# A fused state-space and mixture-of-experts layer on one core: the chunk products, masks and norm in another order

## What is computed

```python
h  = rmsnorm(layernorm(x)) * w_norm_in
z, xx, B, C, dt_raw = split(h @ w_in_proj)          # 256, 256, 8x64, 8x64, 8
xx = silu(causal_conv4(xx) + conv_b)
dt = mean_per_head(softplus(dt_raw @ w_dt + b_dt))  # 8 heads
y  = ssd_scan(xx, dt, B, C, A_log) + xx * D         # state space scan, by chunks
x1 = x + layernorm(x) + rmsnorm(y * silu(z)) * w_norm_out @ w_out_proj
f  = layernorm(x1)
w, i = top_2(softmax(f @ gate_w + gate_b))          # of 4 experts
out = x1 + f + mean_of_2(shared experts(f)) + sum(w * routed experts(f)[i])   # relu, 128->512->128
```

## Time and profile before

| | us |
|---|---|
| median of 3 runs (575.18 to 577.2) | 575.23 |
| the profiled execution's own time | 571.37 |
| its span, first to last instruction | 569.6 |
| one body of the middle (from 322.11 to 387.88 on TensorE) | 65.8 |

### The profile page before, as it was taken

One profiled execution on the slowest core, in us unless ns is written; L12 is line 12 of the kernel. 1 busy time (PEld: TensorE's weight loads), 2 busy tenths in 40 slices (PEclk: granted clock), 3 DMA queues, 4 the chain that ended last, 5 costly groups with the idle time before them and its releaser, 6 DMA issues.

```text
span 569.6 us, 11656 instructions
## 1 busy us (share of the span) xinstructions
PE 541.9 (95%) x3912; PEld 428.5 (75%) x3912; DVE 437.3 (77%) x1037; ACT 355.9 (62%) x767; POOL 173.0 (30%) x232
## 2 busy tenths in 40 slices
PE   8887999999989999999999999999999999899996
PEld 7666778877877777877777777778777778777774
DVE  5868868978699777978778787987778777675654
ACT  4894579547675478636776387745886377752442
POOL 3074405520162203620155201622045211442011
PEclk9989999999999999999999999999999999999999
DMA  6650027200550006500371005600073004500030
GB/s 200 193 152 2 0 73 173 64 1 2 157 167 1 2 6 206 115 1 0 106 162 54 0 0 157 166 0 0 32 201 89 0 0 137 148 25 1 26 72 20
DMA packets 37353, 41.41 MB, mean 73 GB/s; under 512 B 3482, under 2 KB 27716, under 8 KB 37316
## 3 DMA queue, kind: packets, MB, share of 16 engines
q1 hardware_dynamic: 36724, 40.80, 26.1%
q10 hardware_dynamic: 592, 0.15, 0.1%
HBM read 37.79 MB, written 3.15 MB: 72 GB/s over the span
## 4 chain that ended last, share of the span: by engine, by line
PE 48%; DVE 20%; issue 9%; DMA 9%; ACT 8%; POOL 3%; SPq 2%; DVEq 0%; ACTq 0%; POOLq 0%
PE bank L425 7%; DMA grow<-lc_rows 6%; PE bank L427 5%; PE bank L426 5%; PE bank L534 4%; PE bank L639 4%; DVE cv L1122 4%; PE bank L640 4%; PE bank L641 4%; ACT act_h L871 3%; DVE act_l L1269 3%; PE bank L546 2%; PE bank L562 2%; ACT L968 2%; PE bank L556 2%
## 5 line engine op out<-in xcount | busy, mean ns | idle before, releaser
L1269 DVE SCALAR_TENSOR_TENSOR act_l<-bank,act_h 128x512 fp32r<-128x512 f32 x192 | 131.7, 687 | 66.2 <-ACT act_h L871 64.1
L871 ACT ACTIVATE act_h<-bank 128x512 fp32r<-128x512 f32 x192 | 114.3, 596 | 79.4 <-PE bank L427 75.7
L1493 POOL TENSOR_TENSOR late<-late 128x512 f32<-128x512 f32 x31 | 39.8, 1285 | 166.3 <-DVE late L1277 165.7
L425 PE MATMUL bank<-fTl,w1h 128*128 128x512 f32 x192 | 86.9, 452 | 1.2 <-DVE act_l L1269 0.5
L891 ACT ACTIVATE seg<-seg,lneg 128x128 f32<-128x128 f32 x256 | 81.2, 391 | 3.7 <-DMA seg<-lc_rows 3.7
L639 PE MATMUL bank<-act_l,w2h 128*128 128x512 f32 x192 | 77.6, 404 | 1.5 <-DVE act_l L1269 1.5
L640 PE MATMUL bank<-act_h,w2l 128*128 128x512 f32 x192 | 76.0, 396 | 0.0
L427 PE MATMUL bank<-fTh,w1h 128*128 128x512 f32 x192 | 75.7, 394 | 0.0
L641 PE MATMUL bank<-act_h,w2h 128*128 128x512 f32 x192 | 75.6, 394 | 0.0
L426 PE MATMUL bank<-fTh,w1l 128*128 128x512 f32 x192 | 75.5, 393 | 0.0
L1480 POOL TENSOR_TENSOR xw<-xs,seg 128x128 f32<-128x128 f32 x48 | 20.0, 416 | 153.0 <-ACT seg L891 87.5
(11 more groups left out here) (176 smaller groups left out, 1059.3 us busy)
## 6 DMA issues: line engine op xcount, KB each, us to landing
seg<-lc_rows SPq DMA_DIRECT2D x32, 512.0 KB, 4.2
late<-gk_rows SPq DMA_DIRECT2D x8, 1024.0 KB, 9.1
grow<-lc_rows SPq DMA_DIRECT2D x48, 128.0 KB, 4.8
x_in<-L_attn_hidden_dram SPq DMA_DIRECT2D x8, 256.0 KB, 4.1
out_dram<-late SPq DMA_DIRECT2D x8, 256.0 KB, 3.7
late<-L_ffn_sw_dram SPq DMA_DIRECT2D x2, 512.0 KB, 7.2
late<-L_ffn_rw_dram SPq DMA_DIRECT2D x1, 1024.0 KB, 7.7
CT<-L_attn_w_in_proj_dram SPq DMA_DIRECT2D x1, 512.0 KB, 5.4
```

Of the source, the lines that this page charges most:

```text
L425: mm(dst, stat_h, mov_l, start=True, stop=False)
L871: nc.scalar.activation(act_h[:, b % RING, :], HID[b % 2][:], ACT.Relu).then_inc(act_h_ready, 1)
L1269: v_.scalar_tensor_tensor(act_l[:, r, :], HID[b % 2][:], 0.0, f(act_h[:, r, :]), ALU.max, ALU.subtract)\
```

## The change

- TensorE: the gram of chunk 0 stays in slot 13; the gram of chunk c+1 is now issued in step 2 of chunk c, right before the y product of chunk c. The state product moves from step 2 to step 1 (slots 13, 16, 19). Slot 22 holds only `proj(s+1, 0)`.
- VectorE: chunk 0's masked halves stay in slot 13. Chunks 1 and 2 get theirs in step 0 (slots 15, 18), half 0 ahead of `act_low`, half 1 behind it; chunk 3 gets both in slot 21, ahead of `routed_out` and `act_low`. The state update moves to the end of slots 13, 16, 19. The norm's statistics of the next sequence stand ahead of `act_low` of slot 15, its rest behind it; `norm1_apply` moves behind `act_low` and half 1 of slot 18. The copy of B's third block moves from ScalarE to VectorE (slot 5), with a semaphore of its own.
- ScalarE: loses that copy; `growth` of chunk 1 moves from slot 12 to slot 14, behind `decays`.
- GpSimd: in slot 18 the first `add_term` waits for the next sequence's norm (`hn_ready`).
- SyncE: `segments(s, 1)` and `growth_rows(s, 1)` are issued ahead of the store of `older`.
- The opening keeps its own order on VectorE (both halves in step 1, the state in step 2), but takes the new order on TensorE, ScalarE's `growth` included.

```diff
@@ sync
+                    segments(s, 1)
+                    growth_rows(s, 1)
                 if older is not None:
                     sp_eng.wait_ge(out_ready, nth(older, 1, 1))
                     sp_eng.dma_start(out_dram[older], out_t).then_inc(out_stored, 16)
                 if s is not None:
-                    segments(s, 1)
-                    growth_rows(s, 1)
                     growth_rows(s, 2)
@@ tensor
-            def y_product(s, c):
-
+            def state_product(s, c):
                 if c > 0:
                     pe.wait_ge(state_step, nth(s, 8, (2, 5, 8)[c - 1]))
+                pe.wait_ge(btok_ready, nth(s, 3, c + 1))
+                pe.wait_ge(xw_ready, nth(s, 6, 2 * c + 2))
+                for n in range(NP):
+                    ins = mm(MAIN[1][:, n * 64:(n + 1) * 64], btok[:, at(n)], xw[:, n, :, :].rearrange("p t d -> p (t d)"),
+                             start=True, stop=True)
+                ins.then_inc(s_psum, 1)
+
+            def y_product(s, c):
+
+                if c == NCH - 1:
+                    pe.wait_ge(state_step, nth(s, 8, 8))
                 if c < NCH - 1:
...
+                    gram(s, c + 1, None)
...
-                    if b == 0:
+                    if b == 0 and c == NCH - 1:
                         pe.wait_ge(mg_ready, nth(s, 8, 2 * c + 2))
...
-                    if step == 1:
+                    if step == 1 and c == 0:
                         gram(s, c, prev)
-                        if c == NCH - 1 and not is_seq(s, n_seq - 1):
-                            proj(s + 1, 0)
+                    if step == 1 and c < NCH - 1:
+                        state_product(s, c)
+                    if step == 1 and c == NCH - 1 and not is_seq(s, n_seq - 1):
+                        proj(s + 1, 0)
@@ scalar
                         btok_copy(s, c)
-                        if c < NCH - 2:
-                            growth(s, c + 1)
+                        if c == 1:
+                            growth(s, 2)
...
+                    if step == 2 and c == 0:
+                        growth(s, 1)
...
-                    if s is not None and i == 5:
-                        b_copy(s, 2)
@@ vector
+            def third_b_copy(s):
+                dve.wait_ge(proj_psum, made(s, 8))
+                v_.tensor_copy(BT[:, 2, :], MAIN[0][:]).then_inc(b_third_ready, 1)
...
+                        if i in (15, 18, 21):
+                            masked_gram(s, i // 3 - 4, 0)
+                        if i == 15 and not is_seq(s, n_seq - 1):
+                            norm1_stats(s + 1)
+                        if i == 21:
+                            masked_gram(s, 3, 1)
...
+                    if s is not None and i == 5:
+                        third_b_copy(s)
                     if prev is not None and i in (15 + LAG, 19 + LAG):
                         routed_out(prev, (i - 15 - LAG) // 4)
                     if (new := block_at(i, prev, older)) and not (i == 0 and prev is not None):
                         act_low(*new)
...
+                    if s is not None and i in (15, 18):
+                        masked_gram(s, i // 3 - 4, 1)
+                    if s is not None and i in (13, 16, 19):
+                        next_state(s, i // 3 - 4)
+                    if s is not None and i == 15 and not is_seq(s, n_seq - 1):
+                        norm1(s + 1)
+                    if s is not None and i == 18 and not is_seq(s, n_seq - 1):
+                        norm1_apply(s + 1)
@@ gpsimd
+                    if prev is not None and s is not None and i == 16 + LAG and not last:
+                        pool.wait_ge(hn_ready, nth(s + 1, 4, 4))
                     if prev is not None and i in (16 + LAG, 19 + LAG):
                         add_term(prev, (i - 15 - LAG) // 4)
```

More of the change, by code:

```diff
@@ L221, in build @@
         b_ready = sem("b_ready")
+        b_third_ready = sem("b_third_ready")
         c_ready = sem("c_ready")
@@ L470, in proj @@
                     dst = MAIN[j - 10]
-                    last, k = ((b_ready, 3), (b_ready, 4), (xs_ready, 1), (xs_ready, 2))[j - 10]
-                    pe.wait_ge(last, nth(s, 2 if last is xs_ready else 4, k))
+                    last, per, k = ((b_third_ready, 1, 1), (b_ready, 3, 3), (xs_ready, 2, 1), (xs_ready, 2, 2))[j - 10]
+                    pe.wait_ge(last, nth(s, per, k))
                     if j == 12 and not is_seq(s, 0):
@@ L513, in b_tokens @@
                         pe.wait_ge(gate_logits, nth(prev, 4, 4))
-                    pe.wait_ge(b_ready, nth(s, 4, 4))
+                    pe.wait_ge(b_ready, nth(s, 3, 3))
+                    pe.wait_ge(b_third_ready, nth(s, 1, 1))
                     if is_seq(s, 0):
@@ L782, in opening @@
                         b_tokens(0, c, None, None)
-                    gram(0, c, None)
+                    if c == 0:
+                        gram(0, c, None)
                     if c < 2:
@@ L790, in opening @@
                         proj(1, 0)
+                    if c < NCH - 1:
+                        state_product(0, c)
                     y_product(0, c)
@@ L838, in b_copy @@
                 act.wait_ge(proj_psum, made(s, b + 6))
-                nc.scalar.copy(BT[:, b, :], MAIN[(b + 2) % 4][:]).then_inc(b_ready, 1)
+                nc.scalar.copy(BT[:, b, :], MAIN[(b + 2) % 4][:]).then_inc(b_third_ready if b == 2 else b_ready, 1)
             def c_copy(s, b):
@@ L1145, in c_copy @@
                 v_.tensor_copy(CT[:, b, :], MAIN[b][:]).then_inc(c_ready, 1)
-            def attend(s, c, step):
[L1148 to L1155, removed]
-                if step == 2:
[L1158 to L1174, removed]
@@ new lines, in masked_gram @@
+            def masked_gram(s, c, hf):
+                dve.wait_ge(g_psum, nth(s, 8, 2 * c + hf + 1))
+                dve.wait_ge(decay_masked, nth(s, 8, 2 * c + hf + 1))
+                if hf == 0 and (v := nth(s, 4, c)) is not None:
+                    dve.wait_ge(y_psum, v)
+                v_.tensor_tensor(mg[:, hf], MAIN[2 + hf][:].rearrange("p (n l) -> p n l", n=NP), decay(c)[:, hf], ALU.mult)\
+                    .then_inc(mg_ready, 1)
+            def attend(s, c, step):
+                if step == 1 and (c == 0 or is_seq(s, 0)):
+                    masked_gram(s, c, 0)
+                    masked_gram(s, c, 1)
+                if step == 2:
+                    if c < NCH - 1 and is_seq(s, 0):
+                        next_state(s, c)
@@ L1183, in attend, with next_state @@
                     v_.tensor_tensor(yT[:, :, at(c)], yT[:, :, at(c)], szT[:, :, at(c)], ALU.mult).then_inc(yz_ready, 1)
+            def next_state(s, c):
+                first = (0, 2, 5)[c]
+                if c > 0:
+                    dve.wait_ge(grow_ready, nth(s, 3, c))
+                    v_.tensor_tensor(state_m[:], state[:, (c - 1) % 2], grow[:, c % 2, :, P - 1:P].to_broadcast([P, NP, 2 * HD]),
+                                     ALU.mult).then_inc(state_step, 1)
+                    dve.wait_ge(state_step, nth(s, 8, first + 1))
+                    first += 1
+                dve.wait_ge(s_psum, nth(s, 3, c + 1))
+                own = MAIN[1][:, 0:256].rearrange("p (n d) -> p n d", n=NP)
+                for t in range(2):
+                    q, d = slice(64 * t, 64 * t + 64), slice(HD * t, HD * t + HD)
+                    if c == 0:
+                        v_.tensor_copy(state[q, c % 2, :, d], own[q, :, d]).then_inc(state_step, 1)
+                    else:
+                        v_.tensor_tensor(state[q, c % 2, :, d], own[q, :, d], state_m[q, :, d], ALU.add).then_inc(state_step, 1)
+                dve.wait_ge(state_step, nth(s, 8, first + 2))
             def mean_square(s):
@@ L1303, in scan_part @@
                     attend(s, *divmod(i - CHUNKS_FROM, 3))
[L1304 to L1307, removed]
             def body(s, prev, older):
@@ L1365, in opening @@
             def opening():
+                norm1_stats(0)
                 norm1(0)
@@ L1399, in opening @@
                     scan_part(0, i)
+                    if i == 15:
+                        norm1_stats(1)
+                        norm1(1)
+                    if i == 18:
+                        norm1_apply(1)
                     if i == NBLK - 4:
```

11 lines of the change are left out of this document (3 added, 8 removed).

## The result

The changed kernel takes 572.17 us (median of 17 runs, 570.03 to 574.37), the kernel before in the same session 576.86 (17 runs, 571.56 to 582.84). The ratio is 0.9944, interval 0.9918 to 0.9971 (the two medians alone would give 0.9919, at its edge): faster by 0.6%, where 0.9% was forecast. The profiled execution hardly shows it: span 569.2 after 569.6, own time 570.96 after 571.37, where 566.1 was forecast for it.

The account below looks back on a forecast made before the run. TensorE's list order, busy 541.9 of 569.6 us, was taken as the bound. For the profiled execution 571.37 - 5.5 (seven sequences) + 0.2 (opening) = 566.1; as ratio 0.9907, 569.9 us, own range 567.5 to 572.3, 8 in 10 565 to 575.5.

Parts of the forecast that it names:

- own sign of being wrong: State product waits for `btok` or `xw`, or the body shrinks by less than 0.4 or more than 1.2 us.
- Part 5: Norm and GpSimd's delayed expert sum: hn falls from 1.70 to some 1.1 us, hidden in a gap; worth 0.
- the opening: Sequence 0: y delayed by 1.1, ScalarE loses a 0.7 DMA wait; +0.2 us, from -1.5 to +1.5.
- Part 1: Growth leaves slot 12, gram a step ahead: TensorE's wait for `mg` goes, 5.6 us over sequences 1 to 7.
- Part 2: Fewer changes of tile shape on TensorE: 0.4 us a sequence, between 0 and 0.6.
- the walk: Step-by-step timing of TensorE through sequence 5 in the new order: `scan_end` at about 383.15 instead of 383.80.
- Part 3: B's third copy on VectorE: 0.4 to 0.5 gained, waited back at slot 9; 0, at best 0.4 a sequence.
- Part 4: VectorE's tail: `hTl` 0.1 late at slot 22, block 16 waits 0.4 for `routed_out`, between no wait and 1.0.
- the tight place: VectorE's tail at slot 22: `hTl` comes as the slot begins, then `routed_out` behind both halves of `mg`.
- The clock: Opening: TensorE ran at granted 0.50 in 40:41; any shift of idle time may move that.
- Rival 3: `routed_out` behind two halves: VectorE over 1.1 us later before slot 21, block 16 waits 1.5; 578.5 or 579; chance 0.10.
- Rival 2: The wait only changes its name: block 16 waits 1.0, or the first `seg` is late; 573 to 577; chance 0.21.

Follow-up runs that it names:

- e1: Changed kernel without GpSimd's wait for the next sequence's norm in slot 18; 570.14 us, ratio 0.9892 to the kernel before.
- e9: Changed kernel without GpSimd's wait for the norm and with the opening's products in the old order; 567.51 us, ratio 0.9811.
- e3: Kernel before with only growth of chunk 1 moved to slot 14 and the second segments and growth rows issued ahead of the store; 566.67 us, ratio 0.9819.
- e12: The same kernel as e3, measured again; 565.82 us, ratio 0.9787.
- e6: Changed kernel with growth of chunk 1 back in slot 12 and its DMAs behind the store; 583.84 us, ratio 1.0132.
- e4: Changed kernel with the copy of B's third block back on ScalarE; 571.96 us, ratio 0.9919.
- e7: Changed kernel with the opening's TensorE products in the old order, each gram in its own step; 569.13 us, ratio 0.9868.
- e2: As e1, with VectorE's `routed_out` ahead of the two masked halves in slot 21; 569.9 us, ratio 0.9868.

## Why the prediction was right or wrong

The time lies in the stated range and the sign came out, but the mechanism did not: by the prediction's own sign of being wrong (a body that shrinks by less than 0.4) it failed in sequence 5, which it had walked through, 65.77 for 65.76. The forecast's 5.3 us was too much against 3.2 (0.56% of 575.23).

The profiled execution, for which the sum was made, has the account. Forecast were -5.5 us in the bodies and +0.2 in the opening. Measured are -2.86 in bodies 2 to 7 and +2.34 in the opening and body 1. Two steps failed: Part 5, set at nothing, which took 2.7 of the gain (e1 has -5.56 in bodies 2 to 7, the forecast's 5.5), and the opening, set at +0.2. That the timed runs come as near as 0.9944 to 0.9907 is in part luck: there Part 1 gains twice what was forecast and covers what the two failed steps cost. Without these two the runs have 0.9811 (e9), twice the forecast.

- **Part 1** named the right mechanism, and for the profiled execution its size was right: 5.5 us forecast, 5.7 (e3) and 6.1 (e12) measured over bodies 2 to 7, by this part alone. (The `mg` wait stood in six bodies, not seven; sequence 1 had none, and the 5.6 us are the same.) In the timed runs the same edit gains 10 and 12 us. The profile of the kernel before was of a good execution, 571.37 us at a mean granted clock of 0.996; its medians beside the experiments were 576.5 to 578.3, at 0.988 to 0.990, and those of e3 and e12 have 0.995 and 0.997. Over the 40 runs of the kernel before beside the experiments, 0.001 less of mean clock goes with about 0.5 us more, so some 3 of the 10 us and some 5 of the 12 go with the clock (an estimate from these runs). Why the moved growth goes with a higher clock, and whether longer DMA waits make up the rest, is open, since none of the slower executions was profiled. Within the one profile the wait of y for `mg` runs from 0.35 to 1.55. That the DMA wait is behind the late `mg` is shown both ways (e3 and e6).
- **Part 2** counted 0.4 us a body for tile changes. In the profile they are saved (up to slot 22 the walk holds to 0.02 us), but e9, with the new order, and e12, with the old, have bodies of 65.04 and 65.06 and times of 567.5 and 565.8 on one chip. TensorE gives the savings back in waits for VectorE. No net value of the new order is shown.
- **Part 3** was right: 0 net, with the wait moved to slot 9 (the product at 345.83 starts 0.55 behind the one before it, 0.32 more than the usual 0.23, of which the row shows 0.16 as idle time); e4 confirms it by 65.77 for 65.77.
- **Part 4** had `hTl` 0.1 late and block 16 at 0.4 of wait. e1, without Part 5's wait, loses 0.16 and 0.28 there, and its body is 0.70 below the changed kernel's; the forecast's 0.65 was, by its own steps, a forecast of e1.
- **Part 5** is the first step that failed: "worth 0 either way". It cost 0.60 to 0.73 in each of bodies 3 to 6, 2.7 us in the profile and some 3 us by the timed runs of e1 (0.9944 to 0.9892). The text did see `state_m` beside the sum and 0.4 of cost in front of the tight place, and then left it out of the sum. The row it had (0.81) showed an overlap in part; here the overlap was nearly whole: 0.87 more, and 0.43 more on the gating through the pushed CTe (1.42 for e1's 0.99). By the Trainium skill (SBUF — State Buffer, Who interferes with whom), a VectorE instruction with two SBUF inputs contends with a GpSimd instruction that reads SBUF, and one with at most one SBUF input outside the 2-port modes does not. The trace agrees: `act_l`, with one input in PSUM, keeps its 0.68 beside anything. `hn`, with one SBUF input, took 1.70 beside GpSimd and 1.10 alone; whether it ran in a 2-port mode no run here shows.
- **The opening** is the second step that failed. It was set at +0.2 within 1.5; e7 puts it at some 3 to 4 us (0.76%), at least twice the bound. The chain had been named (`mg` releases gram 1, y is later by 1.1), its following waits had not: 1.82 and 1.97 for `mg` before grams 2 and 3, 0.91 for `hTl`. The clock had been named as a risk; what share it has is open.
- **Rivals.** Rival 3's place was right, slot 22, but `hTl` and not `routed_out` held TensorE, for 0.84, short of a loss. Rival 2 is what the profile has in sequences 3, 5 and 6: the wait only changed its name, from `mg` and BT to `hTl` and `act_l`, though by Part 5 and not by the mechanisms that it named.

## What to carry to other kernels

A DMA that a busy engine waits for in its list costs what it holds up behind it; moving the consumer of the late data behind work that has its data was worth 2% here, by a few lines, and more than the profile of one good execution said: look at the mean clock of all timed runs before a wait is sized from one profile. Before an engine is made to wait so that it spares another, look at what it will meet instead, with two-input operations on SBUF first. And when the bound engine's queue is freed of work in front of a chain of another engine, ask for the length of that chain: two orders of TensorE's products, and three of VectorE's slot 21, gave a body of 65.07 within 0.03 us (e1, e2, e3, e9, e12).

## What the runs showed of the hardware

A VectorE operation with two SBUF inputs that started while a GpSimd operation on SBUF was running ended 0.26 to 0.29 us behind that operation, whatever it takes alone (0.41 for 128x256): `state_m` from 371.73 to 373.01 with GpSimd's sum until 372.73, the gating from 374.52 to 375.94 with CTe until 375.66, and so in the kernel before, in e1 (gating 0.99) and in the row of 0.81 of the earlier trace rows, where CTe ended at 39.00. Where VectorE's started first, it kept 0.42 and GpSimd's took 1.55 instead of 1.29.

The spread of the kernel before (571.6 to 582.8) is far wider than that of the changed kernel (570.0 to 574.4) or of e12 (565.3 to 566.7), and its mean granted clock lower (0.988 beside e12's 0.997). In the profiles all falls of the clock but one begin before 60 us. Some follow an idle time of TensorE of some 2 us, but nearly as often the same idle time was followed by none, so that one profile with or without a fall says little of a repair.
